# Four more products by C on GpSimd, its operands set 8 bytes apart, and a new order of the work around them

## The chip, the cores and the metric

The kernel runs on one core of a Trainium2 chip. The metric is the device time of one execution in microseconds (us). The engines that matter here are TensorE (PE in the profile), VectorE (DVE), ScalarE (ACT), GpSimd (POOL) and the queue that issues DMAs (SP). They run side by side and wait for each other on semaphores.

## What is computed

A layer of a state space model on images (8 images, 96 channels, 64x64), then attention and a feed forward layer. The change touches the selective scan alone:

```
dA = exp(dt * A)                     # per channel d (192) and state n (16)
h  = dA * h + (dt * u) * B           # step by step over 4096 places
y  = sum over n of h * C  + D * u    # for 4 directions, k = 0..3
```

Directions 2 and 3 go through the places backwards. `dt` is a softplus of a small projection of `u`; `B` and `C` are other rows of that projection.

## The kernel before

The function is `phase_scan`. The 192 x 16 rows of states make 24 **tiles** of 128 partitions, and the 4096 places are cut into 4 chunks of `T` = 1024 places: 8 images x 4 directions x 4 chunks = 128 **chunks** of 24 tiles. Each engine has its own hand-written order of a chunk (`body`, `run`, `rest`), which is the same for all chunks but for the ends; nothing schedules it at build time.

What happens to tile i of a chunk:

- ACT makes `exp` of it (`expo`, line 888) into one of two PSUM halves `pd[:, i % 2]`, two tiles ahead of the scan.
- GpSimd multiplies `dt * u` by B (`drive`, line 1103) into a ring of four buffers `dBu`. For the six *turned* tiles 9 to 14, ACT scales (line 929) and TensorE transposes (`turn_back`, line 796) instead, and `exp` goes straight into `h`.
- DVE runs the recurrence (`scan`, line 1063), with the last column of the chunk before from `carry`, which ACT saved (line 896).
- The result is multiplied by C. For 12 tiles DVE does it (`weigh`, line 1072), reading `pd`; for the other 12, called kept (each third tile and the turned ones), the scan writes to one of six places of `h`, and GpSimd multiplies there (`weigh`, line 1111), one element beside itself.
- TensorE adds up the states of three tiles at a time (`reduce_states(j)`, line 816, j = 0 to 7) into `py`, which ACT copies out after j = 3 and j = 7 (`copy_y`, line 963).

Woven into this, for the next chunk: the projection (`make_x_dbl` 746, its transposes `turn_b` 754, `make_step` 764), the softplus in ACT steps (`absolute` 935, `exp_abs` 939, `relu` 944, `one_plus` 948, `log` 953), its sum on TensorE (`add_up` 772 to 777), `dt * u` on DVE (`delta_u`, line 1044, after tiles 10 and 20), and its transposes (`turn_du` 784). The table `STEPS` says after which tile ACT does what, `SCALE` and `SCALE_NEXT` how many of the 32 scalings go after which tile. All of it is first in, first out on each engine, so what waits holds up all that is behind it.

In the profile, line 1103 reads `rep` and `BB` (in `shared`), line 1111 reads `h` and `CC` (in `shared`). The tensors `shared`, `rep`, `h` and `dBu` begin at multiples of 16 bytes. A place of `h` has 1025 elements of 4 bytes, so the six places begin at different offsets within 16 bytes; `rep`, `BB` and `CC` rows all begin at offset 0.

Of the kernel before, what the change touches and what calls it, by code (L numbers as in the profile page):

```python
# [17 lines left out]
F32 = mybir.dt.float32  # L18
# [5 lines left out]
L = H * W  # L24
# [354 lines left out]
def phase_scan(nc, a):  # L379

    with ExitStack() as ctx:
# [3 lines left out]
        BK = B * K  # L385

# [17 lines left out]
        BB = a.shared[:, 6 * T:9 * T].rearrange("p (r t) -> p r t", r=3)  # L404
        CC = a.shared[:, 9 * T:13 * T].rearrange("p (r t) -> p r t", r=4)
        hC_shared = a.shared[:, 13 * T:16 * T].rearrange("p (i t) -> p i t", i=3)
# [3 lines left out]
        hC_own = sb("hC", [128, 3, T])  # L410
# [17 lines left out]
        DRIVEN, WEIGHED, TURNED, SCALED = 18, 12, 6, 4 * TB  # L428
# [12 lines left out]
        KEPT = tuple(i for i in range(NS) if TRIPLES[i // 3][1] == 3 or i % 3 == 2)  # L441
# [5 lines left out]
        def kept(i, k):  # L447

            return h[:, KEPT.index(i) % 6, 1:T + 1] if k < 2 else h[:, KEPT.index(i) % 6, 0:T]

        def kept_last(i, k):

            return h[:, KEPT.index(i) % 6, T:T + 1] if k < 2 else h[:, KEPT.index(i) % 6, 0:1]

        def weighted(i, k):

            if is_kept(i):
                return h[:, KEPT.index(i) % 6, 0:T] if k < 2 else h[:, KEPT.index(i) % 6, 1:T + 1]
            slot = place(i) // 3 % 3 * 2 + i % 3
            return hC_own[:, slot, :] if slot < 3 else hC_shared[:, slot - 3, :]  # L460
# [5 lines left out]
        def saved_before(bk, c, i):  # L466

            before = KEPT.index(i) - 6
            if before >= 0 and c < NC - 1:
                return [carries(bk, c, KEPT[before])]  # L470
            return [carries(bk, c - 1, KEPT[before])] if before < 0 and c > 0 else []

        def kept_reduced(n, i):

            before = KEPT.index(i) - 6
            return (n + before // 12) * 8 + KEPT[before % 12] // 3 + 1

        def weighted_reduced(n, i):

            before = place(i) - 9  # L480
            return (n + before // DRIVEN) * 8 + tile_at(before % DRIVEN) // 3 + 1
# [8 lines left out]
        def place(i):  # L490

            j = i // 3
            return (j if j < 3 else j - 2) * 3 + i % 3
# [14 lines left out]
        def weighed_dve(n, i):  # L508

            return n * WEIGHED + place(i) // 3 * 2 + i % 3 + 1  # L510

        def weighed_pool(n, i):

            return n * WEIGHED + (1, 2, 3, 6, 9, 10, 11, 12)[i // 3] - (2 - i % 3 if is_turned(i) else 0)
# [77 lines left out]
        def _(sp):  # L592
# [42 lines left out]
            def load_c(m, s, r):  # L635
                sp.wait_ge(S.bc_stored, done((m + 1) * 16))
                sp.sem_inc(S.passed, 1)
                last = 3 * TRIPLES.index((1, r)) + 2
                if r < 3:
                    sp.wait_ge(S.hc_dve, done(weighed_dve(m - 1, last - 1)))  # L640
                    sp.sem_inc(S.passed, 1)
                sp.wait_ge(S.hc_pool, done(weighed_pool(m - 1, last)))
# [94 lines left out]
        def _(pe):  # L737
# [70 lines left out]
            def reduce_states(n, k, j):  # L808
                if j % 4 == 0:
                    pe.wait_ge(S.y_made, done(n * 2 + j // 4))  # L810
                if not is_turned(3 * j):
                    pe.wait_ge(S.hc_dve, done(weighed_dve(n, 3 * j + 1)))
                pe.wait_ge(S.hc_pool, done(weighed_pool(n, 3 * j + 2)))
# [18 lines left out]
            def body(bk, k, c, left):  # L832
# [4 lines left out]
                reduce_states(n, k, 1)  # L837
                turn_back(bk, c, 9)
                turn_back(bk, c, 10)
                reduce_states(n, k, 2)  # L840
# [5 lines left out]
                turn_back(bk, c, 14)  # L846
                if left:
                    make_step(n + 1, 1)
                skip(n, s, 0)
                reduce_states(n, k, 3)  # L850
# [4 lines left out]
                reduce_states(n, k, 5)  # L855
                if left:
                    turn_du(n + 1, 1)
                reduce_states(n, k, 6)
                if left >= 2:
                    make_x_dbl(n + 2, s)  # L860
                    turn_b(n + 2)
                    make_step(n + 2, 0)
                reduce_states(n, k, 7)
# [3 lines left out]
        def _(act):  # L867
# [107 lines left out]
            for i in range(2):  # L975
# [5 lines left out]
            STEPS = {0: [(absolute, 0)],  # L981
                     1: [(exp_abs, 0)],
                     2: [(relu, 0), (one_plus, 0)],
                     4: [(log, 0)],
                     9: [(copy_delta, 0)],
                     10: [(copy_du, 0)],
                     13: [(absolute, 1), (exp_abs, 1)],
                     14: [(relu, 1), (one_plus, 1)],
# [3 lines left out]
            SCALE = {0: 3, 2: 1, 3: 2, 4: 4, 5: 3, 6: 6}  # L992
            SCALE_NEXT = {20: 4, 21: 4, 23: 5}

            def run(bk, k, c, left, first, steps):
                n, s = bk * NC + c, c % 2
                for i in steps:
# [94 lines left out]
        def _(pool):  # L1092
# [24 lines left out]
            def body(bk, k, c, left):  # L1117
                n = bk * NC + c
                for j in range(8):
                    if is_turned(3 * j):  # L1120
                        for i in range(3 * j, 3 * j + 3):
                            weigh(n, k, i)
                    else:
                        p = place(3 * j) + 3
                        if left or p < DRIVEN:
                            for g in range(3):
                                drive(n, c, p + g)
                        weigh(n, k, 3 * j + 2)
# [670 lines left out]
def program(nc, a):  # L1799

    names = SEMAPHORES.split()
    with ExitStack() as ctx:
# [6 lines left out]
        a.shared = ctx.enter_context(nc.sbuf_tensor("shared", [128, 4 * L], F32))  # L1809
# [70 lines left out]
```

## Time and profile before

| | |
|---|---|
| median of three runs | 11818.88 us (11809.55 to 11828.68) |
| the profiled execution | 11838.25 us, of which the span in the trace is 11836.4 us |
| stage of the scan, 128 chunks | 849 to 10256 us of the span |
| busy in the span | PE 78%, DVE 90%, ACT 72%, GpSimd 75% |

The profile is one execution. A row of a timeline gives the start in us of the span, the time taken, engine, line, operation and tiles, and in brackets the idle time before it and who ended it. Instructions of one engine overlap slightly, so the time from start to start is what adds up. In rows that give stretches, PEclk is the granted clock of TensorE: 1.00 is 2.4 GHz and 0.50 is 1.2 GHz.

### The profile page before, as it was taken

The numbers are of one execution on the slowest core, as the hardware profiler recorded it, in microseconds if no ns is written. First come the engines' busy times: TensorE is split into PE (matmuls) and PEld (weight loads), VectorE is DVE, ScalarE is ACT, GpSimd is POOL, SyncE is SP. The second block draws the span as 40 slices with busy tenths as digits, with TensorE's granted clock in tenths as the row PEclk, the third lists the DMA queues.
The fourth block names the chain that finished last, engine by engine and source line by source line (L and its number), as shares of the span: only waits on it lengthen the run. The fifth ranks groups of instructions, "written<-read, shape, count | busy, mean of one in ns | idle before, by whom it ended". The sixth has DMA issues, their size and how long they took to land. (4 is left out here: it accounts for less than half of the span.)

```text
span 11836.4 us, 143180 instructions
## 1 busy us (share of the span) xinstructions
PE 9269.9 (78%) x34584; PEld 3297.3 (28%) x34584; DVE 10602.0 (90%) x6847; ACT 8553.0 (72%) x13829; POOL 8919.1 (75%) x3956
## 2 busy tenths in 40 slices
PE   8877777777777777777777777777777777588888
PEld 2322222222222222222222222222222222133333
DVE  7769999999999999999999999999999999866565
ACT  6767777777777777777777777777777777455555
POOL 0019998999899989998999899989999999521210
PEclk9988888888888888888888888888888888799898
DMA  3347777777777777777777777777777777644341
GB/s 106 118 131 183 182 184 178 183 183 184 178 182 184 182 174 183 184 179 175 187 183 183 177 184 182 178 177 184 183 182 182 187 180 180 147 111 99 93 106 48
DMA packets 577591, 1948.34 MB, mean 165 GB/s; under 512 B 106615, under 2 KB 111639, under 8 KB 562199
## 3 DMA queue, kind: packets, MB, share of 16 engines
q1 hardware_dynamic: 573714, 1938.65, 68.6%
q8 instruction: 265, 4.34, 0.2%
q14 instruction: 536, 4.38, 0.1%
q10 hardware_dynamic: 3076, 0.97, 0.1%
HBM read 1532.38 MB, written 406.85 MB: 164 GB/s over the span
## 5 line engine op out<-in xcount | busy, mean ns | idle before, releaser
L1103 POOL TENSOR_TENSOR dBu<-rep,shared 128x1024 f32<-128x1024 f32 x2304 | 5373.1, 2357 | 886.7 <-DMA rep<-dd_dram 832.1
L1111 POOL TENSOR_TENSOR h<-h,shared 128x1024 f32<-128x1024 f32 x1536 | 3310.3, 2162 | 717.5 <-DVE h L1063 700.7
L888 ACT ACTIVATE pd<-rep,a_now 128x1024 f32<-128x1024 f32 x2304 | 2566.7, 1114 | 761.1 <-DVE h L1063 463.0
L816 PE MATMUL py<-h,fold 128*32 128x512 f32 x6144 | 2613.6, 722 | 163.6 <-ACT y L963 163.6
L1063 DVE TENSOR_TENSOR_SCAN pd<-pd,carry,dBu 128x1024 f32<-128x1024 f32 x1152 | 2697.4, 2341 | 23.4 <-ACT pd L888 23.4
L816 PE MATMUL py<-hC,fold 128*32 128x512 f32 x3072 | 1366.7, 806 | 557.9 <-POOL h L1111 557.0
L929 ACT ACTIVATE shared<-shared,turned_b 128x192 f32<-128x192 f32 x4096 | 1528.1, 442 | 15.5 <-ACT shared L916 5.4
L816 PE MATMUL py<-shared,fold 128*32 128x512 f32 x3072 | 1409.9, 836 | 126.9 <-POOL h L1111 126.6
L1063 DVE TENSOR_TENSOR_SCAN h<-pd,carry,dBu 128x1024 f32<-128x1024 f32 x576 | 1349.5, 2343 | 103.3 <-ACT carry L896 53.1
L796 PE MATMUL pd<-eye,shared 128*128 128x128 f32 x6144 | 859.2, 288 | 597.9 <-DVE h L1063 402.4
L1063 DVE TENSOR_TENSOR_SCAN h<-h,carry,pd 128x1024 f32<-128x1024 f32 x576 | 1306.7, 2323 | 12.8 <-PE pd L796 6.9
L1072 DVE TENSOR_TENSOR hC<-pd,shared 128x1024 f32<-128x1024 f32 x768 | 940.5, 1225 | 81.5 <-DVE pd L1063 28.8
L1072 DVE TENSOR_TENSOR shared<-pd,shared 128x1024 f32<-128x1024 f32 x768 | 940.6, 1225 | 46.2
L796 PEld LDWEIGHTS pd<-eye,shared 128*128 128x128 f32 x6144 | 701.5, 145 | 913.0 <-DVE h L1063 501.3
L1063 DVE TENSOR_TENSOR_SCAN pd<-pd,dBu 128x1024 f32<-128x1024 f32 x384 | 876.1, 2282 | 47.8 <-issue 34.4
L888 ACT ACTIVATE h<-rep,a_now 128x1024 f32<-128x1024 f32 x768 | 846.7, 1140 | 15.2 <-ACT carry L896 10.3
L1782 POOL TENSOR_TENSOR shared<-shared 96x1024 f32<-96x1024 f32 x56 | 140.1, 2530 | 946.3 <-DMA shared<-y_dram 946.3
L764 PE MATMUL pp<-xdbl,w_dt 38*96 38x512 f32 x1024 | 716.2, 836 | 58.3 <-ACT turned_b L909 57.4
L916 ACT ACTIVATE shared<-pp 128x768 f32<-128x768 f32 x256 | 207.5, 810 | 638.5 <-PE pp L784 638.5
L816 PEld LDWEIGHTS py<-hC,fold 128*32 128x32 f32 x3072 | 230.7, 130 | 1476.3 <-POOL h L1111 688.4
L816 PEld LDWEIGHTS py<-h,fold 128*32 128x32 f32 x6144 | 449.8, 123 | 584.4 <-issue 466.3
L896 ACT ACTIVATE carry<-pd 128x1 f32<-128x1 f32 x1152 | 192.8, 167 | 577.1 <-DVE hC L1072 320.8
(174 smaller groups left out, 14520.0 us busy)
## 6 DMA issues: line engine op xcount, KB each, us to landing
rep<-dd_dram SPq DMA_DIRECT2D x1024, 768.0 KB, 12.3
shared<-bc_dram SPq DMA_DIRECT2D x3584, 128.0 KB, 5.8
u<-u_dram SPq DMA_DIRECT2D x128, 768.0 KB, 7.8
dd_dram<-LG SPq DMA_DIRECT2D x256, 384.0 KB, 4.6
dd_dram<-RL SPq DMA_DIRECT2D x256, 384.0 KB, 3.3
y_dram<-y SPq DMA_DIRECT2D x256, 384.0 KB, 7.3
shared<-y_dram SPq DMA_DIRECT2D x63, 1536.0 KB, 15.9
u_dram<-shared SPq DMA_DIRECT2D x32, 1536.0 KB, 7.5
```

The lines of the kernel that those rows point to most:

```text
L764: last = mm(pp[0:HALF, t2(t)], w_dt[:, half * HALF:(half + 1) * HALF], xdbl[:, t2(t)], start=True, stop=True)
L796: last = nc.tensor.transpose(pd[:, i % 2, block_of(q)], turned_dbu[:, q, half * 3 + g, :, :], eye128[:, :])
L816: last = mm(py[32 * g:32 * g + 32, t2(t)], fold[:, :], weighted(3 * j + g, k)[:, t2(t)], start=(j % 4 == 0), stop=(j % 4 == 3), skip_group ...
L888: go(dst, rep[:, half, 0, g, :], ACT.Exp, scale=a_now[:, column(i)]).then_inc(S.exped, 1)
L896: go(carry[:, i:i + 1], kept_last(i, k) if is_kept(i) else pd[:, i % 2, last_of(k)], ACT.Identity).then_inc(S.carried, 1)
L916: go(turned_du[:, :, 3 * half:3 * half + 3, :], pp[:, :].rearrange("p (q x) -> p q x", x=128)[:, :, 0:HALF].rearrange("p q (g d) -> p q g ...
L929: go(turned_dbu[:, q, :, j, :], turned_du[:, q, :, :], ACT.Identity, scale=turned_b[:, s, q, j:j + 1]).then_inc(S.scaled, 1)
L1063: v.tensor_tensor_scan(turned(state(i, k), k), turned(decay, k), turned(drive, k), first, ALU.mult, ALU.add).then_inc(S.scanned, 1)
L1072: v.tensor_tensor(weighted(i, 0), pd[:, i % 2, :], CC[:, r, :], ALU.mult).then_inc(S.hc_dve, 1)
L1103: nc.gpsimd.tensor_tensor(dBu[:, ring(c, p), :], rep[:, half, 1, g, :], BB[:, r, :], ALU.mult).then_inc(S.dbu, 1)
L1111: nc.gpsimd.tensor_tensor(turned(weighted(i, k), k), turned(kept(i, k), k), turned(CC[:, r, :], k), ALU.mult).then_inc(S.hc_pool, 1)
L1782: last = nc.gpsimd.tensor_tensor(Y[:, 0, c * T:(c + 1) * T], Y[:, 0, c * T:(c + 1) * T], Y[:, 2, c * T:(c + 1) * T], ALU.add)
```

## The change

- **Offsets.** `BB` moves by 2 elements (8 bytes), `CC` and the product buffers by 4, `shared` grows by 8 elements. A place of `h` has 1028 elements, and forward the scan writes from element 3 and the product from element 2 (backwards the other way round), so all places have the same offset.
- **Split.** `DVE_TILES` = 0, 3, 4, 6, 15, 18, 19, 21: DVE multiplies these 8 by C, GpSimd the other 16.
- **Places.** `h` has 8 places in place of 6; DVE's products have 4 in place of 6.
- **Order.** The orders of GpSimd, TensorE and ACT are written anew. On TensorE `reduce_states` 1 and 2 go behind other transposes, 5 goes behind `turn_du`, and 6 behind `make_x_dbl`, `turn_b` and `make_step` of the chunk after next. On ACT `absolute` and `exp_abs` of the first half go one tile later, `exp_abs` now right behind `copy_y`; `relu` of the second half goes one tile earlier.

```
-        KEPT = tuple(i for i in range(NS) if TRIPLES[i // 3][1] == 3 or i % 3 == 2)
+        DVE_TILES = (0, 3, 4, 6, 15, 18, 19, 21)
+        KEPT = tuple(i for i in range(NS) if i not in DVE_TILES)
...
-        BB = a.shared[:, 6 * T:9 * T].rearrange("p (r t) -> p r t", r=3)
-        CC = a.shared[:, 9 * T:13 * T].rearrange("p (r t) -> p r t", r=4)
+        BB = a.shared[:, 6 * T + 2:9 * T + 2].rearrange("p (r t) -> p r t", r=3)
+        CC = a.shared[:, 9 * T + 4:13 * T + 4].rearrange("p (r t) -> p r t", r=4)
...
-        h = sb("h", [128, 6, T + 1])
+        h = sb("h", [128, PLACES, T + 4])
...
-            return h[:, KEPT.index(i) % 6, 1:T + 1] if k < 2 else h[:, KEPT.index(i) % 6, 0:T]
+            return h[:, KEPT.index(i) % PLACES, 3:T + 3] if k < 2 else h[:, KEPT.index(i) % PLACES, 2:T + 2]
...
-            STEPS = {0: [(absolute, 0)],
-                     1: [(exp_abs, 0)],
-                     2: [(relu, 0), (one_plus, 0)],
+            STEPS = {1: [(absolute, 0)],
+                     2: [(exp_abs, 0), (relu, 0), (one_plus, 0)],
...
-                     13: [(absolute, 1), (exp_abs, 1)],
-                     14: [(relu, 1), (one_plus, 1)],
+                     12: [(absolute, 1), (exp_abs, 1)],
+                     13: [(relu, 1)],
+                     14: [(one_plus, 1)],
```

TensorE in the middle of a chunk, from the transposes of tile 13 to the sum of tiles 9 to 11 (`pd` is turned tiles, 764 `make_step`, 804 the skip term, 816 the sums). Before:

```order
L796 MATMUL pd<-eye,shared 128x128 x8
L790 REGISTER_ALU
L796 MATMUL pd<-eye,shared 128x128 x8
L764 MATMUL pp<-xdbl,w_dt 96x512 x2
L802 ISA
L804 MATMUL py<-u,w_skip 96x512 x2
L816 MATMUL py<-h,fold 32x512 x6
```

Now (the same lines are 799, 767, 807 and 821):

```order
L799 MATMUL pd<-eye,shared 128x128 x8
L767 MATMUL pp<-xdbl,w_dt 96x512 x2
L793 REGISTER_ALU
L799 MATMUL pd<-eye,shared 128x128 x8
L805 ISA
L807 MATMUL py<-u,w_skip 96x512 x2
L818 REGISTER_ALU
L816 REGISTER_ALU x2
L821 MATMUL py<-hC,fold 32x512
L821 MATMUL py<-h,fold 32x512 x2
```

The step goes ahead of the transposes of tile 14, and the sum of tiles 6 to 8 (the last two rows, and again for the other half of the places) stands ahead of that of 9 to 11.

TensorE at the end of a chunk, from `make_x_dbl` on to the last sum of the chunk, that of tiles 21 to 23. Before:

```order
L746 MATMUL pp<-u,w_x 38x512 x4
L751 REGISTER_ALU
L754 MATMUL pp<-eye,xdbl 128x38 x8
L764 MATMUL pp<-xdbl,w_dt 96x512 x2
L812 REGISTER_ALU
L816 MATMUL py<-shared,fold 32x512 x2
L816 MATMUL py<-h,fold 32x512
```

Now:

```order
L749 MATMUL pp<-u,w_x 38x512 x4
L754 REGISTER_ALU
L757 MATMUL pp<-eye,xdbl 128x38 x8
L767 MATMUL pp<-xdbl,w_dt 96x512 x2
L818 REGISTER_ALU x2
L816 REGISTER_ALU
L821 MATMUL py<-shared,fold 32x512 x2
L821 MATMUL py<-h,fold 32x512
L821 MATMUL py<-shared,fold 32x512 x2
L821 MATMUL py<-h,fold 32x512
L818 REGISTER_ALU
L816 REGISTER_ALU x2
L821 MATMUL py<-hC,fold 32x512
L821 MATMUL py<-h,fold 32x512 x2
```

Two sums stand behind the step now: that of tiles 18 to 20 (`shared` twice, `h` once) and, behind it, that of 21 to 23; before it was the last alone.

ACT around `copy_y` of the chunk before (963, now 968), after tile 2. Before:

```order
L888 ACTIVATE pd<-rep,a_now 128x1024
L961 REGISTER_ALU
L962 ISA
L963 ACTIVATE y<-py 96x1024
L942 ISA
L944 ACTIVATE RL<-pp,b_dt 96x1024
L948 ACTIVATE W<-E 96x1024
L929 ACTIVATE shared<-shared,turned_b 128x6x32
```

Now:

```order
L893 ACTIVATE pd<-rep,a_now 128x1024
L967 ISA
L968 ACTIVATE y<-py 96x1024
L944 ACTIVATE E<-E 96x1024
L947 ISA
L949 ACTIVATE RL<-pp,b_dt 96x1024
L953 ACTIVATE W<-E 96x1024
L934 ACTIVATE shared<-shared,turned_b 128x6x32 x2
```

One step of softplus (944) and one more scaling (934) now stand between `copy_y` and the next `exp` of a tile, that of tile 5.

## Rows read from the trace of the kernel before

**Rows 1.** The page, busy time, share of the span and instructions of each engine

```profile
PE 9269.9 (78%) x34584; PEld 3297.3 (28%) x34584; DVE 10602.0 (90%) x6847; ACT 8553.0 (72%) x13829; POOL 8919.1 (75%) x3956
```

**Rows 2.** Stretches: length, busy PE, PEld, DVE, ACT, POOL, then PEclk, DMA share, GB/s

```profile
849.00:10256.00 9407.00, 7242.45 (x28577) 2563.06 (x28580) 9049.02 (x4858) 7141.50 (x11774) 8635.37 (x3834) 0.87 0.77 181
...
3631.74:3703.89 72.15, 55.31 (x224) 19.80 (x224) 71.09 (x39) 56.67 (x99) 67.73 (x30) 0.91 0.78 183
7992.85:8068.27 75.42, 58.40 (x224) 20.06 (x224) 71.09 (x39) 57.04 (x99) 67.76 (x30) 0.84 0.76 179
```

**Rows 3.** DVE idle before its scans: releaser, us in total, times

```profile
  ACT pd L888: 98.8, 49
  ACT carry L896: 79.4, 31
...
  PE pd L796: 12.8, 24
```

**Rows 4.** Timeline of DVE, scans of tiles 1 to 3 of a chunk

```profile
3635.45 2.35 DVE L1063 TENSOR_TENSOR_SCAN pd<-pd,carry,dBu 128x1024 f32<-128x1024 f32 x1
...
3638.98 2.34 DVE L1063 TENSOR_TENSOR_SCAN h<-pd,carry,dBu 128x1024 f32<-128x1024 f32 x1
3641.24 2.33 DVE L1063 TENSOR_TENSOR_SCAN pd<-pd,carry,dBu 128x1024 f32<-128x1024 f32 x1
```

**Rows 5.** GpSimd by line: duration ns min/median/max

```profile
L1111 POOL TENSOR_TENSOR h<-h,shared x1536: 1907/2186/2404, 852.9 to 10252.0; 128x1024 f32<-128x1024 f32 x192
...
L1103 POOL TENSOR_TENSOR dBu<-rep,shared x2304: 2329/2356/2407, 832.5 to 10240.4; 128x1024 f32<-128x1024 f32 x192
```

**Rows 6.** Timeline of GpSimd, tile 5 of a backward chunk, tiles 2 to 5 of a forward one

```profile
1519.71 1.93 POOL L1111 TENSOR_TENSOR h<-h,shared 128x1024 f32<-128x1024 f32 x1
1521.60 7.00 POOL L1103 TENSOR_TENSOR dBu<-rep,shared 128x1024 f32<-128x1024 f32 x3
...
3641.40 2.34 POOL L1111 TENSOR_TENSOR h<-h,shared 128x1024 f32<-128x1024 f32 x1 [0.56 <-DVE h L1063]
3643.70 6.98 POOL L1103 TENSOR_TENSOR dBu<-rep,shared 128x1024 f32<-128x1024 f32 x3
3650.78 2.00 POOL L1111 TENSOR_TENSOR h<-h,shared 128x1024 f32<-128x1024 f32 x1
```

**Rows 7.** Timeline of PE over the end of a chunk at 3703.89

```profile
3694.73 1.32 PE L784 MATMUL pp<-eye,RL 96*128 96x96 f32 x8 [3.90 <-DVE RL L1044]
...
3705.43 3.73 PE L764 MATMUL pp<-xdbl,w_dt 38*96 38x512 f32 x4 [0.46 <-ACT turned_b L909]
3709.09 1.07 PE L816 MATMUL py<-shared,fold 128*32 128x512 f32 x2
...
3711.64 0.79 PE L816 MATMUL py<-shared,fold 128*32 128x512 f32 x2
```

**Rows 8.** Timeline of ACT behind it, and DVE's scan of tile 5

```profile
3714.54 1.00 ACT L963 ACTIVATE y<-py 96x1024 f32<-96x1024 f32 x1
...
3720.49 2.34 DVE L1063 TENSOR_TENSOR_SCAN h<-pd,carry,dBu 128x1024 f32<-128x1024 f32 x1
```

**Rows 9.** Timeline of PE in the middle of two chunks, and DVE's wait in the second

```profile
3671.24 1.95 PE L764 MATMUL pp<-xdbl,w_dt 38*96 38x512 f32 x4
3673.12 1.96 PE L804 MATMUL py<-u,w_skip 96*96 96x512 f32 x4
3675.01 1.92 PE L816 MATMUL py<-h,fold 128*32 128x512 f32 x12
...
8032.32 2.80 PE L764 MATMUL pp<-xdbl,w_dt 38*96 38x512 f32 x4
...
8046.13 2.35 DVE L1063 TENSOR_TENSOR_SCAN h<-pd,carry,dBu 128x1024 f32<-128x1024 f32 x1 [3.28 <-ACT carry L896]
```

**Rows 10.** Stretches of rows 7 and 9, columns as in rows 2

```profile
3705.50:3709.10 3.60, 3.60 (x7) 0.90 (x7) 3.38 (x3) 2.72 (x6) 3.60 (x3) 0.50 1.03 200
...
3670.30:3677.00 6.70, 6.63 (x28) 2.30 (x28) 6.58 (x3) 4.30 (x5) 6.53 (x4) 1.00 1.01 215
```

More of the change, by code:

```diff
@@ L466, in saved_before @@
         def saved_before(bk, c, i):
[L468 removed]
+            before = KEPT.index(i) - PLACES
             if before >= 0 and c < NC - 1:
@@ L637, in load_c @@
                 sp.sem_inc(S.passed, 1)
[L638 to L642, printed above, removed]
+                last = 3 * TRIPLES.index((1, r))
+                for i in range(last, last + 3):
+                    if not is_kept(i):
+                        sp.wait_ge(S.hc_dve, done(weighed_dve(m - 1, i)))
+                        sp.sem_inc(S.passed, 1)
+                sp.wait_ge(S.hc_pool, done(weighed_pool(m - 1, last + 2)))
                 sp.sem_inc(S.passed, 1)
@@ L810, in reduce_states @@
                     pe.wait_ge(S.y_made, done(n * 2 + j // 4))
-                if not is_turned(3 * j):
-                    pe.wait_ge(S.hc_dve, done(weighed_dve(n, 3 * j + 1)))
-                pe.wait_ge(S.hc_pool, done(weighed_pool(n, 3 * j + 2)))
+                for i in range(3 * j, 3 * j + 3):
+                    if is_kept(i):
+                        pe.wait_ge(S.hc_pool, done(weighed_pool(n, i)))
+                    else:
+                        pe.wait_ge(S.hc_dve, done(weighed_dve(n, i)))
                 for t in range(2):
@@ L991, in _, with run @@
                      20: [(copy_du, 1)]}
-            SCALE = {0: 3, 2: 1, 3: 2, 4: 4, 5: 3, 6: 6}
-            SCALE_NEXT = {20: 4, 21: 4, 23: 5}
-            def run(bk, k, c, left, first, steps):
+            SCALE = {0: 3, 2: 2, 3: 3, 4: 2, 5: 6, 6: 2, 7: 1}
+            SCALE_NEXT = {20: 5, 21: 3, 22: 2, 23: 3}
+            def run(bk, k, c, left, first, span):
                 n, s = bk * NC + c, c % 2
-                for i in steps:
+                for i in span:
                     if c < NC - 1:
@@ L1118, in body @@
                 n = bk * NC + c
[L1119 to L1128, printed above, removed]
+                drive(n, c, 3)
+                drive(n, c, 4)
+                weigh(n, k, 1)
+                weigh(n, k, 2)
+                drive(n, c, 5)
+                drive(n, c, 6)
+                drive(n, c, 7)
+                drive(n, c, 8)
+                weigh(n, k, 5)
+                drive(n, c, 9)
+                drive(n, c, 10)
+                weigh(n, k, 7)
+                drive(n, c, 11)
+                weigh(n, k, 8)
+                weigh(n, k, 9)
+                weigh(n, k, 10)
+                weigh(n, k, 11)
+                weigh(n, k, 12)
+                weigh(n, k, 13)
+                weigh(n, k, 14)
+                drive(n, c, 12)
+                drive(n, c, 13)
+                weigh(n, k, 16)
+                weigh(n, k, 17)
+                drive(n, c, 14)
+                drive(n, c, 15)
+                drive(n, c, 16)
+                drive(n, c, 17)
+                weigh(n, k, 20)
+                if left:
+                    drive(n, c, 18)
+                    drive(n, c, 19)
+                weigh(n, k, 22)
+                if left:
+                    drive(n, c, 20)
+                weigh(n, k, 23)
             chunk_loop(pool, body)
```

43 lines of the change are left out of this document (22 added, 21 removed).

## The prediction

> **What bounds the kernel now.** I read the busy shares first. DVE is busy 90% of the span, more than any other [rows 1], and in the stage of the scan, 9407 us or 73.5 us for each of its 128 chunks, 9049 us [rows 2]. An undisturbed chunk takes 72.15 us, with DVE busy for 71.1 of them [rows 2]: there DVE is the bound and waits for nobody. Other chunks take 75.42 with the same work. The idle time before the scans says how much that is: 98.8 and 79.4 us ended by ACT, 12.8 by PE [rows 3], together 191 us or 1.5 us for each chunk. So a chunk is DVE's work and 1.5 us of waits. GpSimd is busy 67.7 of 72.15 us, which leaves no room for four more products as they are.
>
> From start to start, a kept tile costs DVE 2.26 us and a tile with a product 3.53 [rows 4]; 3.58 on the mean, since 72.15 is 12 of these, 12 at 2.25 and two `delta_u` at 1.11.
>
> **GpSimd's times.** The multiplication by C has a shortest time of 1907 ns and a median of 2186, the one by B none under 2329 [rows 5]. The timeline shows two values, not a spread: tile 5 of a backward chunk takes 1.93, of a forward one 2.00, tile 2 takes 2.34 [rows 6]. Over the chunks that I followed, places 1, 2 and 5 of `h` always have the short time and places 0, 3 and 4 the long one. With 1025 elements to a place, the first begin in the other 8 bytes of 16 than C does (offsets 2, 3 and 2 against 0), the others in the same (1, 0 and 1). `rep` and `BB` both begin at 0 and have the long time. The change gives all places the offset of place 2, which is in the trace, and B the offset 2 against 0. From start to start a long one costs 2.33 (6.98 for three) and a short one 1.89 to 1.95 (from 1519.71 to 1521.60, from 3650.78 with 2.00 less the usual overlap) [rows 6]. So GpSimd's chunk becomes 34 x 1.92 = 65.3 us, with 63.5 for the least and 66.5 for the most. That multiplications by B become short too is the one part that no row shows; their operands differ from those of the short products only in which of the two is displaced, and I give it nine in ten.
>
> GpSimd is slower than DVE at this: the trace has 1.9 to 2.35 us against 1.22 for the same product. The Trainium skill says the same (GPSIMD Engine Reference, section 3.1), and gives about 2.5 cycles for each element as the floor with two inputs, since both are read through one port; 1024 elements at 1.2 GHz would be 2.13 us, an estimate from that page. The trace disagrees, with 1.907. By that rule the multiplications by B would end at 2.13, GpSimd's chunk at 34 x 2.13 = 72.5, and nothing would be gained.
>
> **DVE.** Four tiles less with a product: 4 x (3.58 - 2.26) = 5.3 us; an unhindered chunk is 66.9 us. With 128 chunks that is 675 us, if all else keeps pace. GpSimd does: its new order gives each buffer over 2 us or more before the scan that needs it, when I lay both orders side by side with these times. The places are no limit either: tile 16 is the earliest to need a sum of its own chunk (that of 6 to 8), and 3 has to wait for the old sum of 18 to 20, taken up below.
>
> **The end of a chunk is what I doubt.** PE's chain there starts with DVE's `delta_u` after tile 20. Its transposes start at 3694.73, the step at 3705.43, 10.7 us later; the last sum runs from 3709.09 to 3712.43 [rows 7], 8.5 us after the chunk's start at 3703.89. `copy_y` takes it at 3714.54 [rows 8], so 2.1 us are to spare. After the change, tiles 21 to 23 and `delta_u` take 1.11 + 3.58 + 2 x 2.26 = 9.2 us (10.5 now), so the chain starts 8.05 us before the chunk ends instead of 9.2. The step then starts at 2.65, and two sums follow it in place of one. The clock during the step is 0.50, 1.2 GHz, after PE had waited [rows 10], and the step takes 3.66, a sum 3.34 [rows 7]. At that clock the last sum ends at 2.65 + 3.66 + 2 x 3.34 = 13.0; at 2.4 GHz, with 1.88 and 1.9 [rows 9], at 8.3. I take 12.2, since the sums themselves may lift the clock before the last is done, as in the half of the last sum in rows 7 (its last group takes 0.79 us, not 1.07).
>
> ACT wants it after the `exp` of tile 4, at 8.2 + 1.1 = 9.3. From `copy_y` to the scan of tile 5 there then stand 0.9 (`copy_y`), 3 x 0.97 (`exp_abs`, `relu`, `one_plus`), 0.7 (two scalings), 0.25 (saves), 1.1 (`exp`) and 0.4 to the scan, 6.3 us. Today it is 5.95, of which part is slack [rows 8]. DVE wants tile 5 at 15.2. So it waits 0.4 us if the sum is early, 4.2 if all is at 1.2 GHz, and with 12.2 + 0.15: **3.4 us**. Tile 3's product waits for the first of the two sums, which ends at 9.65 where it is wanted at 10.6: free. From there on ACT is full up to tile 9 (32 scalings less 13 made before), and PE has stood still and may be at 1.2 GHz at the transposes of tiles 10 and 11 with a sum between them: **0.5 us**, between 0 and 1.5, of the size that a single wait for PE has today (12.8 us in 24) [rows 3]; the end at 1.5 is three of them.
>
> **The middle of a chunk.** Tile 17 needs `exp`, which stands behind `copy_y` of the first half, which needs the sum of tiles 9 to 11. From the end of scan 11 PE has then two sets of transposes (2 x 1.03), the step (1.88), the skip term (1.89) and two sums (3.8): 9.6 us, and from there to the scan 3.85 (`copy_y`, `one_plus`, saves, `exp`; `relu` is out of the way now), 13.5. DVE comes from there to tile 17 in 4 x 2.25 + 3.58 + 2.26 - 2.32 = 12.5. **1.0 us** of waiting in each chunk, even at 2.4 GHz. Before, this chain just fitted at 2.4 GHz [rows 9, 10] and cost 3.28 us where the clock fell (the step took 2.80 at 8032.32) [rows 9]. What the fall will cost then I put at **0.8 us** for the mean chunk, against 1.5 now: PE's long idle time before this stretch is gone, since the sum of tiles 3 to 5 and the step stand between the transposes now.
>
> **The sum.** 66.9 + 3.4 + 0.5 + 1.0 + 0.8 = 72.6 us, against 72.15 + 1.5 = 73.65. 1.05 us less, 128 times: 135 us, and 1.1%. Against the profiled execution, 11838 - 135 = 11703. The median of the runs is 19 us under it: 11684, of which I make 11680. Four fifths of what DVE saves are paid back in waits, if I am right, and one fifth remains.
>
> **Rivals.**
>
> *The cover holds.* If PE is at 2.4 GHz at the chunk's end, or its chain is faster than I lay it, `copy_y` costs 0.4 and not 3.4. Then a chunk is 66.9 + 0.4 + 0.3 + 1.0 + 0.5 = 69.1, 4.5 less: 580 us, 11240 us. For it: every term of the wait is a small difference of long chains, and with shorter chunks PE has less idle time. Against it: 0.50 in rows 10 after a shorter idle time than will be there.
>
> *The middle breaks, slower.* The chain in the middle has one more sum than before ahead of `copy_y`. If the clock falls there, its 7.5 us of step, skip and sums take up to twice that, and 3.3 to 6.6 us are added to the 1.0. It decides the sign from 1.85 us on the mean chunk instead of 0.8, so if about two chunks in five are hit with 4.6. With half of them hit, and 4.2 at the chunk's end: 66.9 + 4.2 + 0.5 + 1.0 + 2.5 = 75.1, 1.45 more, 12005 us. For it: 75.42 us chunks with 0.84 [rows 2] show that the clock does fall there. Against it: PE stood still ahead of it, and will less.
>
> *The operands do not do it.* If the products by B stay at 2.33: 18 x 2.33 + 16 x 1.92 = 72.7 us for GpSimd, which becomes the bound; with the hand-overs between it and DVE, 73 to 75 us, 11730 to 11990, say 11840. The 2.13 of the skill's page would end in the same place.
>
> **How the numbers follow.** The forecast, 11480 to 11800, has 0.45; the cover 0.25; the middle 0.17; the operands 0.08; the last 0.05 are for a give-back that just eats the gain. 0.2% of the time, 24 us, is about what a measurement of this kernel tells from no change. Faster is the first two, 0.70; slower the middle and half of the operands, 0.21; the same 0.09. The range reaches into the first rival to 11300 and into the second to 11930, with about 0.1 left out on either side.
>
> **What would show it.** The step that all rests on is GpSimd: lines 1108 and 1116 near 1.93 to 2.00 us, without a second value. DVE should have 1024 products of 1.22 us. Its idle time before scans should grow from 1.5 to some 5 or 6 us for each chunk, ended by ACT, in two places: before tile 5, with ACT having waited for PE's last sum at `copy_y`, and before tile 17. If chunks are near 69 us and `copy_y` waits for nothing, the first rival is right; if the wait before tile 17 is over 4 us in half of the chunks and the clock low there, the second; if DVE waits for `dBu`, the third. I would be wrong altogether if DVE were held by an engine that I have with room: SP's loads of C, or GpSimd's last product of a chunk.

## The result, and the profile after

| | before | changed |
|---|---|---|
| median of four runs each, us | 11822.52 (11809.55 to 11828.68) | 11701.33 (11682.28 to 11725.06) |
| ratio | | 0.9895 (0.9877 to 0.9912) |
| span of the profiled execution, us | 11836.4 | 11685.8 |

121 us less, 1.05%. The forecast was 11680, in a range of 11480 to 11800. Lines move by 5: the scan is 1068 now, DVE's product by C 1077, GpSimd's products 1108 and 1116, the sums 821, `copy_y` 968.

The page's first part, answering to [rows 1]: DVE has lost 566 us of work, and GpSimd, with 512 products more, 147 us.

```profile
PE 9207.4 (79%) x34584; PEld 3443.5 (29%) x34584; DVE 10036.1 (86%) x6335; ACT 8437.5 (72%) x13829; POOL 8772.1 (75%) x4468
```

GpSimd by line, duration in ns min/median/max, answering to [rows 5]. The products by B have come from 2356 to 1997 on the median, and those by C, of which half took 2.33 us and more, are all short:

```profile
L1108 POOL TENSOR_TENSOR dBu<-rep,shared x2304: 1986/1997/2077, 834.0 to 10106.9; 128x1024 f32<-128x1024 f32 x192
L1116 POOL TENSOR_TENSOR h<-h,shared x2048: 1917/1987/2026, 844.0 to 10116.5; 128x1024 f32<-128x1024 f32 x187
```

DVE's idle time before its scans (releaser, us, times), answering to [rows 3]: 664 us, where it was 231 (191 ended by ACT and PE, as in the prediction, and 40 "issue").

```profile
  ACT pd L893: 418.9, 265
  POOL dBu L1108: 120.6, 67
  PE pd L799: 55.3, 93
  ACT carry L901: 47.4, 78
  issue: 21.5, 33
```

Sorted by tile, 381 us of it, 3.0 for each chunk, stand before tile 5: 289.2 under ACT's `pd` and 92.0 under GpSimd's `dBu`. One such chunk begins at 5264.94. TensorE at its start, with the step, the sum of tiles 18 to 20 and the last sum (the rows from 5275.50 on), answering to [rows 7]:

```profile
5256.78 1.51 PE L787 MATMUL pp<-eye,RL 96*128 96x96 f32 x8 [4.27 <-DVE RL L1049]
...
5268.66 3.73 PE L767 MATMUL pp<-xdbl,w_dt 38*96 38x512 f32 x4 [1.25 <-ACT turned_b L914]
5272.32 1.07 PE L821 MATMUL py<-shared,fold 128*32 128x512 f32 x2
...
5274.88 0.78 PE L821 MATMUL py<-shared,fold 128*32 128x512 f32 x2
5275.50 0.59 PE L821 MATMUL py<-hC,fold 128*32 128x512 f32 x1
...
5276.78 0.59 PE L821 MATMUL py<-hC,fold 128*32 128x512 f32 x1
```

ACT behind it, from `copy_y` to `exp` of tile 5, answering to [rows 8]:

```profile
5277.54 1.02 ACT L968 ACTIVATE y<-py 96x1024 f32<-96x1024 f32 x1 [2.58 <-PE py L821]
5278.46 1.05 ACT L944 ACTIVATE E<-E 96x1024 f32<-96x1024 f32 x1
5279.41 1.10 ACT L949 ACTIVATE RL<-pp,b_dt 96x1024 f32<-96x1024 f32 x1
5280.41 1.05 ACT L953 ACTIVATE W<-E 96x1024 f32<-96x1024 f32 x1
5281.35 0.79 ACT L934 ACTIVATE shared<-shared,turned_b 128x192 f32<-128x192 f32 x2
...
5282.32 1.12 ACT L893 ACTIVATE pd<-rep,a_now 128x1024 f32<-128x1024 f32 x1
```

And GpSimd's four products 5 to 8, whose first has ended by 5277.9, with DVE's scan of tile 5:

```profile
5275.87 7.87 POOL L1108 TENSOR_TENSOR dBu<-rep,shared 128x1024 f32<-128x1024 f32 x4
...
5283.81 2.35 DVE L1068 TENSOR_TENSOR_SCAN h<-pd,carry,dBu 128x1024 f32<-128x1024 f32 x1 [3.12 <-POOL dBu L1108]
```

The sum ends at 5277.4, 12.4 us into the chunk; ACT has waited 2.58 us for it and needs 6.3 us more until the scan. The row blames GpSimd, but its product for tile 5 had been ready for 5.9 us: it is ACT's `exp`, which ended at 5283.44. In all 30 waits before tile 5 that are put down to GpSimd, ACT's `exp` ended 0.2 to 0.4 us before the scan began, so the 92 us are of the same wait.

Stretches, columns as in [rows 2]: that chunk, its step at the clock's lower level, 1.2 GHz, its middle (tile 12 to 17) and that of the chunk at 3012.44, one of two in which the clock fell there:

```profile
5264.94:5336.82 71.88, 55.85 (x225) 21.21 (x224) 66.74 (x36) 55.66 (x98) 65.98 (x35) 0.88 0.78 184
5268.66:5272.39 3.73, 3.73 (x7) 1.03 (x10) 3.57 (x3) 3.70 (x9) 3.73 (x3) 0.50 1.04 199
5302.43:5315.60 13.17, 11.56 (x61) 4.41 (x62) 12.53 (x7) 9.85 (x15) 12.16 (x7) 1.00 0.80 172
3050.52:3066.98 16.46, 14.85 (x61) 5.62 (x62) 12.64 (x8) 10.28 (x17) 13.65 (x7) 0.79 0.92 185
```

Below, "hit" is such a chunk: over 1.5 us more than its least between the scans of tiles 12 and 17. I count them among the 119 chunks that don't begin a batch of 16, the last chunk left out (all hits have a clock under 1.00 there): 31 before, 2 after.

### The profile page after: what moved, and what is told of

Same layout as the page of the kernel before. It is cut to its first block and busy times, and to the rows that moved or that the text cites. A ratio compares the mean times of both kernels' runs of the same rounds, so it can differ in the third digit from the quotient of the medians.

```text
span 11685.8 us, 144402 instructions
## 1 busy us (share of the span) xinstructions
PE 9207.4 (79%) x34584; PEld 3443.5 (29%) x34584; DVE 10036.1 (86%) x6335; ACT 8437.5 (72%) x13829; POOL 8772.1 (75%) x4468
## 5 line engine op out<-in xcount | busy, mean ns | idle before, releaser
L1108 POOL TENSOR_TENSOR dBu<-rep,shared 128x1024 f32<-128x1024 f32 x2304 | 4552.5, 1998 | 886.2 <-DMA rep<-dd_dram 833.5
L1116 POOL TENSOR_TENSOR h<-h,shared 128x1024 f32<-128x1024 f32 x2048 | 4020.7, 1972 | 728.6 <-DVE h L1068 728.0
L821 PE MATMUL py<-h,fold 128*32 128x512 f32 x8192 | 2447.8, 701 | 214.9 <-ACT y L968 214.9
L1068 DVE TENSOR_TENSOR_SCAN h<-pd,carry,dBu 128x1024 f32<-128x1024 f32 x960 | 2242.4, 2344 | 409.7 <-ACT pd L893 280.0
L1068 DVE TENSOR_TENSOR_SCAN pd<-pd,carry,dBu 128x1024 f32<-128x1024 f32 x768 | 1795.8, 2338 | 0.1
L1068 DVE TENSOR_TENSOR_SCAN h<-pd,dBu 128x1024 f32<-128x1024 f32 x320 | 729.2, 2284 | 139.5 <-ACT pd L893 88.7
L787 PE MATMUL pp<-eye,RL 96*128 96x96 f32 x2048 | 298.1, 307 | 559.5 <-DVE RL L1049 554.5
L1068 DVE TENSOR_TENSOR_SCAN pd<-pd,dBu 128x1024 f32<-128x1024 f32 x256 | 585.4, 2287 | 66.0 <-ACT pd L893 50.2
L775 PE MATMUL pp<-W,neg 97*96 97x512 f32 x1024 | 545.5, 614 | 106.5 <-ACT W L953 106.5
L968 ACT ACTIVATE y<-py 96x1024 f32<-96x1024 f32 x256 | 260.7, 1019 | 473.1 <-PE py L821 473.0
```

The costliest lines, as they stand in the source:

```text
L775: mm(pp[0:HALF, t2(t)], neg[:, :], W1[:, t2(t)], start=True, stop=False)
L787: last = nc.tensor.transpose(pp[:, q * 128:q * 128 + HALF], du[:, block_of(q)], eye)
L821: last = mm(py[32 * g:32 * g + 32, t2(t)], fold[:, :], weighted(3 * j + g, k)[:, t2(t)], start=(j % 4 == 0), stop=(j % 4 == 3), skip_group ...
L968: go(y[:, :], py[0:HALF, :], ACT.Identity).then_inc(S.y_made, 1)
L1068: v.tensor_tensor_scan(turned(state(i, k), k), turned(decay, k), turned(drive, k), first, ALU.mult, ALU.add).then_inc(S.scanned, 1)
L1108: nc.gpsimd.tensor_tensor(dBu[:, ring(c, p), :], rep[:, half, 1, g, :], BB[:, r, :], ALU.mult).then_inc(S.dbu, 1)
```

## The experiments

My theory: GpSimd was made shorter by the offsets alone; DVE's work came down, and 3.0 us of what that saves are paid back before tile 5, because two sums now stand behind TensorE's step. Ratios are to the kernel before as it was measured beside each run, with 95% intervals; its median moved between 11823 and 11831 us, so a difference of two medians below is good to some 10 us. Waits and counts of hits are of the one profiled execution of each kernel.

| kernel | median us | ratio |
|---|---|---|
| changed | 11701 | 0.9895 |
| e3, kernel before with the offsets alone | 11823 | 0.9997 (0.9984 to 1.001) |
| e4, changed, B in the same half | 11856 | 1.0021 (1.0012 to 1.0031) |
| e1, changed, sums 5 and 6 back | 11497 | 0.9713 (0.9697 to 0.9729) |
| e2, changed, `exp_abs` early | 11645 | 0.9834 (0.9813 to 0.9855) |
| e7, e1 and e2 | 11450 | 0.9684 (0.9661 to 0.9706) |
| e5, changed, `copy_y` behind tile 5 | 11560 | 0.9780 (0.9756 to 0.9804) |
| e9, e1 and e5 | 11631 | 0.9836 (0.9816 to 0.9857) |
| e6, changed, sums 1 and 2 back | 12021 | 1.0158 (1.0137 to 1.0179) |
| e10, e7, first `copy_y` later | 11529 | 0.9745 (0.9723 to 0.9768) |
| e11, e7, 16 products added | 11661 | 0.9861 (0.9839 to 0.9883) |
| e12, e7, 8 products added | 11500 | 0.9730 (0.9705 to 0.9755) |
| e13, e12, 8 more at the end | 11468 | 0.9701 (0.9676 to 0.9725) |

### Is it the offsets, and does GpSimd bound?

The kernel before with the new offsets of `BB`, `CC`, the product buffers and `h`, and nothing else:

```
-        BB = a.shared[:, 6 * T:9 * T]
+        BB = a.shared[:, 6 * T + 2:9 * T + 2]
...
-        h = sb("h", [128, 6, T + 1])
+        h = sb("h", [128, 6, T + 4])
```

> The kernel before, with nothing but the offsets of the change: the split stays 12 to 12, and so do the orders and the six places. My theory, that the halves of the 16 bytes in which GpSimd's two operands begin set its time, and that GpSimd bounds nothing before the change: its products all take 1.9 to 2.1 us, its busy time falls from 8635 to near 7400 us in the scan's stage, and the time stays where it was, within 0.3% of 11820. A rival, that a shorter GpSimd also takes waits from DVE: up to 100 us less.

Its GpSimd rows, columns as above, then the scan's stage, columns as in [rows 2]:

```profile
L1103 POOL TENSOR_TENSOR dBu<-rep,shared x2304: 1986/1998/2013, 832.0 to 10208.5; 128x1024 f32<-128x1024 f32 x192
...
L1111 POOL TENSOR_TENSOR h<-h,shared x1536: 1909/1982/2005, 852.6 to 10221.3; 128x1024 f32<-128x1024 f32 x192
```

```profile
849.00:10256.00 9407.00, 7205.67 (x28580) 2559.88 (x28580) 9070.01 (x4867) 7138.56 (x11773) 7541.09 (x3834) 0.87 0.78 181
```

1094 us less of GpSimd's work than in [rows 2], and no time. As expected: it was not on the path. Hits are 25 where they were 31, and DVE's idle time before scans is 201 us where it was 231. The other way round, the changed kernel with B alone in the half of the other operand:

```
-        BB = a.shared[:, 6 * T + 2:9 * T + 2]
+        BB = a.shared[:, 6 * T:9 * T]
```

> The changed kernel with B alone moved back to offset 0, the offset of the other operand. My theory: the products by B take 2.33 us again and those by C 1.95 to 2.0, GpSimd's chunk is 18 x 2.33 + 16 x 1.97 = 73.5 us and it becomes the bound; DVE waits for dBu in every chunk, and the time is 11750 to 12000, say 11850. The rival, that the place of C alone sets both times or that the cause is not the offset: products by B stay near 2.0 and the time stays at 11700.

Its products by B, and the stage up to 10000:

```profile
L1108 POOL TENSOR_TENSOR dBu<-rep,shared x2304: 2327/2356/2464, 834.4 to 10254.9; 128x1024 f32<-128x1024 f32 x192
```

```profile
849.00:10000.00 9151.00, 7065.37 (x27805) 2645.29 (x27804) 8247.69 (x4225) 6847.88 (x11478) 9021.04 (x4223) 0.86 0.77 181
```

Two elements of offset are worth 155 us here. The products by B are at 2356 again, those by C stay at 1986, and GpSimd is busy 98.6% of the stage: it is the bound, 73.6 us a chunk. The prediction put this rival at 11840; it came at 11856. That DVE would be seen waiting for `dBu` was wrong: its idle time is 580.1 us under ACT's `pd`, before tiles 5 and 1, and 84.5 under `dBu`. GpSimd's lateness comes to it, at least in part, over TensorE's sums: they wait for GpSimd's products 126.0 us in 60 waits, where it was 47.1 in 10, ACT's wait for the projection behind one of them is 312.0 us where it was 189.5, and the last sum ends 13.9 us into the mean chunk and not 12.7.

### Is it the last sum that tile 5 waits for?

```
+                reduce_states(n, k, 5)
                 if left:
                     turn_du(n + 1, 1)
-                reduce_states(n, k, 5)
+                reduce_states(n, k, 6)
                 if left >= 2:
                     make_x_dbl(n + 2, s)
                     turn_b(n + 2)
                     make_step(n + 2, 0)
-                reduce_states(n, k, 6)
```

> The changed kernel with the sums 5 and 6 on TensorE where they stood before the change: sum 5 ahead of the transposes of dt * u, sum 6 right behind them and ahead of the projection. My theory, that DVE waits 3.0 us for each chunk before tile 5 because the last sum of the chunk before ends 12.4 us into the chunk, behind two others: that sum now ends near 9.7, and the wait falls to 0.4 to 0.7 us. 128 x 2.4 is 300 us less than the changed kernel, near 11400. A rival, that ACT is just full there and the sum only the last to be named: the wait moves to the next tile and the time stays near 11700. A second, that with the projection behind two sums its own result comes later than tile 1 of the next chunk wants it: the gain is halved, near 11550, with DVE waiting before tile 1 or 3 instead.

The same chunk of this kernel begins at 5162.10. The last sum follows the step at once:

```profile
5166.15 3.72 PE L767 MATMUL pp<-xdbl,w_dt 38*96 38x512 f32 x4 [1.25 <-ACT turned_b L914]
...
5172.37 0.63 PE L821 MATMUL py<-hC,fold 128*32 128x512 f32 x1
...
5173.16 1.02 ACT L968 ACTIVATE y<-py 96x1024 f32<-96x1024 f32 x1 [0.71 <-PE py L821]
...
5179.42 2.35 DVE L1068 TENSOR_TENSOR_SCAN h<-pd,carry,dBu 128x1024 f32<-128x1024 f32 x1 [1.24 <-ACT pd L893]
```

It ends 10.9 us into the chunk and not 12.4, and DVE waits 1.24 us, not 3.12. Over all chunks 156 us are left before tile 5 of 381: 226 less and not 300, since the sum at 1.2 GHz ends 1.2 us later than I had it. The time fell by 204, to 11497 and not to 11400: the waits before tiles 1, 17 and 14 grew by 33, 22 and 17 us, and hits rose from 2 to 16. So the second rival was right in a small part.

The next run leaves the sums where the change put them, and moves a step of ACT:

```
-            STEPS = {1: [(absolute, 0)],
-                     2: [(exp_abs, 0), (relu, 0), (one_plus, 0)],
+            STEPS = {1: [(absolute, 0), (exp_abs, 0)],
+                     2: [(relu, 0), (one_plus, 0)],
```

> The changed kernel with the first half's exp_abs after tile 1 again, ahead of copy_y, and not behind it. My theory: ACT stands still from 10.0 to 12.6 us of a chunk, waiting for the last sum, and exp_abs fits in there. One step of 0.95 us less lies between the sum and exp of tile 5, so the wait before tile 5 falls from 3.0 to near 2.05 us; 128 x 0.95 is 120 us less, near 11580. The rival, that ACT's work up to tile 9 bounds this part whatever its order: nothing, 11700.

From start to start tile 4 to 5 takes 5.70 us on the mean, not 6.57: 0.87 for each chunk, 110 us. But the time fell by 56 only (72 by the ratios), to 11645 and not to 11580. Hits rose from 2 to 17 of 119, and in the profiled execution the waits before tiles 11, 14, 16 and 17 grew by 17, 20, 12 and 31 us. So the step off the chain did what was expected, and about half of it or more was given back in the middle.

Both edits together:

> Sums 5 and 6 back as in the run with the sums alone (11497), and exp_abs of the first half ahead of copy_y as in the run with that alone (57 us less than the changed kernel). If the two act on one chain, from the last sum to exp of tile 5, the second takes 0.95 us or what is left of the wait: 60 to 110 us less than 11497, near 11410. If they act on different waits they add up to 11440. If the wait that remains before tile 5 in the run with the sums is not this chain, 11497.

11450, a little over the 11410 to 11440 that I had, and the best of all: 3.2% under the kernel before and 2.1% under the changed one. 71.9 us are left before tile 5 (50.5 under ACT's `pd`, 15.9 under TensorE's `py`, 4.1 under `dBu`, 1.5 "issue"), and the mean chunk takes 70.46 us. Again the time fell by less than the removed wait, 252 of 309 us: hits are 34 now. ACT takes the last sum without waiting for it here (0.03 us on the mean, 2.6 in the changed kernel), so what is left before tile 5 isn't the sum's any more.

### Is the place of the copy all that matters?

```
-                    if i == 2 and not first:
+                    if i == 3 and not first:
                         copy_y(n - 1, 1)
```

> The changed kernel with the copy of the old sums (copy_y of the second half) one tile later on ACT, so behind exp of tile 5 and not ahead of it. TensorE's order is as in the changed kernel. My theory, that the wait before tile 5 is nothing but that chain from the last sum over copy_y to exp: the wait of 3.0 us goes, and 0 to 0.5 comes back at tile 6 or behind it, since copy_y then starts near 12.6 as before and exp of tile 6 has 2.3 us more; 128 x 2.5 is 320 us less, near 11380. The rival, that ACT is full between tile 2 and tile 9 and the order in it does not matter: the wait turns up before tiles 6 to 11 and the time stays over 11600.

No wait is left before tile 5 (3.51 us from start to start), all 381 us gone, but the time fell by 142, to 11560 and not to 11380. DVE's idle time of this kernel:

```profile
  ACT pd L893: 215.0, 293
  PE pd L799: 135.0, 124
  ACT carry L901: 105.3, 78
  issue: 28.1, 46
  PE py L821: 15.2, 12
```

By tile, 88.9 us stand before tile 9 (12.2 in the changed kernel), 57.2 before 14 (1.6), 129.6 before 17 (52.5), 82.4 before 1 (56.7), 41.1 before 6 (none), and hits are 39. There is one `py` for both halves. So the next chunk's first sum can't start before `copy_y` has read it, and behind it in TensorE's order stand `add_up` and the transposes of tile 9: TensorE's sums wait 569.7 us for `copy_y`, where it was 388.3. My theory had the wait right and what lies behind it wrong.

> Both at once: sums 5 and 6 where they stood before the change, and copy_y of the second half behind exp of tile 5. The run with the sums alone still had 157 us of waits before tile 5, 1.2 us for each chunk (the last sum ended 10.9 us into chunk 61, since TensorE ran at 1.2 GHz). My theory: those go too, 11497 less 130 to 157 us, near 11350. If ACT or the projection's own chain (88 us of waits before tile 1) bounds, 11450 to 11500.

With the sum early as well it is slower than with either of the sums' or the copy's place alone (11497, 11560), and slower than either case that I had expected. TensorE's waits in this kernel, us in total, times, longest, from 849 to 10000 us:

```profile
PE py L821 <- ACT y L968: 788.8, 227, 10.5
...
PE pp L749 <- DMA u<-u_dram: 127.1, 81, 3.8
```

The first was 288.2 in the kernel with the sums alone, the second 41.2. `u` is loaded by SP when `skip` has been computed; the later `copy_y`, the later `skip`, the later `u`, and DVE waits 147 us before tile 1 (90 with the sums alone). That this chain of hand-overs is the cause I read from the order of the code and from these waits; no run tests it.

### The middle

```
+                reduce_states(n, k, 1)
                 turn_back(bk, c, 9)
                 turn_back(bk, c, 10)
-                reduce_states(n, k, 1)
+                reduce_states(n, k, 2)
                 turn_back(bk, c, 11)
...
-                reduce_states(n, k, 2)
```

> The changed kernel with sums 1 and 2 on TensorE where they stood before the change: 1 ahead of the transposes of tile 9, 2 between those of tiles 10 and 11. My theory for the wait before tile 17 (0.4 us for each chunk), that the sum of tiles 6 to 8 stands in the chain from scan 11 to copy_y of the first half: it goes, 50 us less; but transposes of tiles 11 and 9 come 2 to 3.5 us later, behind the sums, and DVE's wait for pd by TensorE before tiles 9 and 11 (0.4 us for each chunk) grows to 1 to 2. Together 11700 to 11850. The rival, that TensorE has the room before tile 9: near 11650.

No wait is left before tile 17, as I had it, and 405.5 us stand before tile 11, 369.6 of them under TensorE's `pd` (48.6 and 42.1 in the changed kernel). I gave these sums 1 to 2 us for each chunk; they cost 3.2, and the time, 12021, lies outside my 11700 to 11850. The old place is 2.7% worse. The clock is under 1.00 between tiles 12 and 17 in 35 of the 119 chunks of this kernel, and none of them is a hit: a lower clock by itself doesn't make one.

```
-                    if i == 14:
+                    if i == 15:
                         copy_y(n, 0)
```

> The kernel with sums 5 and 6 back and exp_abs early (11450), and copy_y of the first half one tile later, behind exp of tile 17 and no longer ahead of it. In that kernel DVE still waits 90 us before tile 17 for ACT's carry and 30 us for its exp. My theory: both waits are the chain over the sum of tiles 9 to 11 and copy_y to exp of tile 17; they go, and 60 to 120 us with them, to 11330 to 11390. The rival, learnt from the run in which copy_y of the second half went one tile later: the next sum on TensorE and add_up behind it wait for the copy, and the time comes back before tiles 21 to 1: 11450 or more.

The rival was right: tile 17's 119 us are gone, but 51.3 came before `delta_u`, 121.9 us stand before tile 1 where it was 64.4, and 35.0 before tile 23 where it was 6.8; 79 us more in all.

Now the clock. In some chunks it falls behind the transposes of tiles 11 and 12, of `dt * u` and of tile 13. Products that nobody reads (`fill`) go in between:

```
                 turn_back(bk, c, 12)
+                fill(8)
                 if left:
                     turn_du(n + 1, 0)
+                fill(8)
                 turn_back(bk, c, 13)
```

> The kernel with sums 5 and 6 back and exp_abs early (11450), and 16 products of 128x128 by fold added on TensorE, whose result nobody reads: 8 behind the transposes of tile 12 and 8 ahead of those of tile 13, where TensorE stands still for 1.4 and 1.5 us. In that kernel 34 chunks lose 3.9 us each between tiles 12 and 16, with a granted clock of 0.79 there and not 1.00, which is 1.0 us for the mean chunk. If the clock falls there because TensorE stands still in these gaps, the 34 become few and the time falls by 80 to 130 us, to 11320 to 11370. If it falls for what was before tile 9, or by itself, nothing is gained, and the products that do not fit the gaps cost up to 1 us a chunk: 11450 to 11570.

> As the run with 16 added products, with 4 and 4 of them in place of 8 and 8. There 8 took 1.93 us where TensorE had 1.4 to 1.5 us of room, the granted clock between tiles 12 and 16 was 1.00 in every chunk and no chunk lost over 1.5 us there, but DVE waited 208 us before tile 13 for transposes that came too late. 4 take 0.97 us and fit. If what holds the clock is that TensorE is at work in these two gaps, half of it may do: the 34 chunks that lost 3.9 us become few, nothing waits before tile 13, and the time is 11450 less 80 to 130 us, near 11340. If it takes all 16, the hits stay and the time is 11430 to 11470.

Tile 12 to 17, columns as in [rows 2]: a hit and the next chunk of e7.

```profile
3704.46:3720.85 16.39, 14.77 (x61) 5.60 (x62) 12.43 (x7) 10.25 (x17) 13.69 (x8) 0.79 0.88 185
3776.62:3789.78 13.16, 11.51 (x61) 4.40 (x62) 12.52 (x7) 10.23 (x17) 12.15 (x7) 1.00 0.82 176
```

A chunk with 16 products (e11):

```profile
3917.05:3932.92 15.87, 14.40 (x88) 6.76 (x86) 12.85 (x8) 10.92 (x17) 12.20 (x7) 1.00 0.86 181
```

And one with 8 (e12):

```profile
3860.46:3874.78 14.32, 12.85 (x74) 5.38 (x73) 12.86 (x7) 10.91 (x17) 12.21 (x7) 1.00 0.94 194
```

Of 34 hits none is left, with 16 products or with 8, and the granted clock is 1.00 there in every chunk. So the half of my expectations on the clock held, and the half on the time did not: e11 takes 211 us more than e7 (11661, where even my rival said 11570 at most), with 225 us of waits before tile 13 and 73 before tile 14, and e12 takes 50 us more, 11500 where I had 11340 or at most 11470. With 8 products the stretch takes 14.25 us on the mean, against 14.09 in e7. TensorE's timeline in that good chunk of e7, and then in the chunk with 8 products, shows why:

```profile
3773.20 1.97 PE L799 MATMUL pd<-eye,shared 128*128 128x128 f32 x16
3775.00 0.83 PE L787 MATMUL pp<-eye,RL 96*128 96x96 f32 x8
3776.75 1.09 PE L799 MATMUL pd<-eye,shared 128*128 128x128 f32 x8 [0.93 <-DVE h L1068]
```

```profile
3858.96 1.06 PE L805 MATMUL py<-eye,fold 128*32 128x128 f32 x8
3859.95 0.88 PE L787 MATMUL pp<-eye,RL 96*128 96x96 f32 x8
3860.76 1.06 PE L805 MATMUL py<-eye,fold 128*32 128x128 f32 x8
3861.75 1.09 PE L799 MATMUL pd<-eye,shared 128*128 128x128 f32 x8
```

The gaps of 1.4 and 1.5 us in my expectations were misread: ahead of the transposes of `dt * u` (787) there is none, ahead of those of tile 13 one of 0.93. The two groups of 4 products (8 matmuls each, 0.99 us from start to start) need 1.98 us, where 0.93 is free. So the transposes of tile 13, which start 0.13 us behind the scan of tile 12 (at 3776.62) in e7, start 1.29 behind it (at 3860.46) in e12, and that delay costs about what the hits had cost, 1.0 us for the mean chunk. By this sum one group alone would about fit; that wasn't tried.

The last run adds two groups at the chunk's end:

> As the run with 4 and 4 added products, and 4 more behind the projection (make_x_dbl) and 4 ahead of the step at the chunk's end, where TensorE stands still for 2.0 and 1.7 us before it takes 3.7 us for the step and 3.6 us for the last sum at 1.2 GHz. If the clock holds there as it did in the middle, the step and the sum take 1.9 us each, the last sum ends 3 us earlier, and the waits left before tiles 5 and 1 (60 and 54 us) mostly go: 60 to 110 us less than with 4 and 4. If the clock is low there for the copies that TensorE waits for at that place whatever it does, the same time, or up to 60 us more since the products delay turn_b.

One chunk of it begins at 5155.45. Its step, its last sum and ACT's `copy_y` behind them:

```profile
5159.27 1.95 PE L767 MATMUL pp<-xdbl,w_dt 38*96 38x512 f32 x4 [0.26 <-ACT turned_b L923]
...
5162.47 0.59 PE L826 MATMUL py<-hC,fold 128*32 128x512 f32 x1
...
5166.60 1.00 ACT L977 ACTIVATE y<-py 96x1024 f32<-96x1024 f32 x1
```

The clock did as I hoped: it is 0.98 over the step in the mean chunk (0.57 in e12), the step takes 2.0 us, and the last sum ends 8.0 us into the chunk and not 10.9. The waits did not: ACT comes to `copy_y` at 11.4 us (11.5 in e12), in both without waiting for the sum, 62 us stay before tile 5 (70 in e12) and 87 before tile 1 (85). So with the sums back and `exp_abs` early it is ACT's own work that tile 5 waits for, and a faster TensorE takes next to nothing off that wait. The time falls by 33 us from e12, half of the least that I expected and not where I expected it, and it doesn't beat e7.

## Why the prediction was right, point by point

- **GpSimd's offsets: right.** B became short too, the part that no row showed. I took 1.92 us from start to start; it is 1.96 by B (5264.26, 5266.22) and 1.92 by C, so a chunk is about 66 and not 65.3 (65.98 busy in the chunk shown), inside my bounds. The prediction's offsets of the places are those of the forward directions. Backwards the operands are read from their last element, and the halves are those of that element: place 1, read from offset 0 against 3, takes 1.93 us on the median, and place 3, read from 2 against 3, takes 2.35. Counted from the lowest address, both would come out the other way round. All 1536 products by C of the kernel before fit this.
- **The skill's rule.** GpSimd's two-input product took 1.99 us on the median, with its two operands in different halves, and 2.36 in the same. The floor of some 2.5 cycles for each element in the Trainium skill (GPSIMD Engine Reference, section 2.1, Instruction dispatch; section 3.1, which the prediction names for it, has some 2.6) would be 2.13 us at 1.2 GHz, an estimate from that page; the trace disagrees in all 4352 products, of which the longest took 2.08.
- **DVE: right in what is left, too large in what is saved.** With every wait over 0.15 us taken out, the mean chunk is 67.0 us, where I had 66.9. With 5.2 of idle time before scans (664 by 128, where I had 5.7) and 0.3 before its products this makes the mean chunk's 72.5. But the same measure gives 71.6 before, and waits of 2.0, where I had 72.15 and 1.5: I left out the 40 us of "issue" and 29 before products, and took the 72.15 of one chunk, with 0.24 of waits in it, for the mean chunk's own work. So the saving was 4.5 us and not 5.3, and the waits grew by 3.5 and not by 4.2. The two errors cancel, which is luck.
- **Before tile 5: right in place and cause, 3.4 expected, 3.0 measured.** The last sum ended at 12.4 in the chunk shown (12.7 in the mean chunk), where I had 12.2, and the clock rose during the first of the two sums (5274.88 is the first row of it that is shorter), as I had supposed it might. That it came out so near is in part luck: the step started 3.7 us into the chunk and not 2.65, since `turn_b` and the step waited 1.41 and 1.25 us for ACT, and the two sums took 5.0 us and not 5.9. From `copy_y` to the scan I had 6.3 us, and it took 6.3. e1, e2 and e5 each took the wait, or a part of it, away at another place of the same chain.
- **Tiles 8 to 11: right.** 0.5 expected, 71 us in 128 chunks measured, 49 of them before tile 11.
- **Tile 17: too large.** 1.0 expected, 0.4 measured (52.5 us). That the chain is there, e6 and e10 show: each takes the wait away at another end.
- **The clock in the middle: too large.** I put 0.8 on it, with the reason that the idle time before it is gone; it is 2 hits of 3 us, nearly nothing. The reason isn't shown: e1, e2, e7 and e5 have the same order of TensorE in the middle, and 16, 17, 34 and 39 hits.
- **What I did not have:** 0.4 us before tile 1 (`copy_x_dbl` waits for the projection, which now stands behind a sum), 0.2 before tile 23, and 0.3 before tile 15 (six chunks, the first of a batch). With 0.2 before tile 0 and 0.3 before DVE's products, both much as before, they make 1.5 us, against 1.7 that I had too much: that the mean chunk is 72.5 where the sum gave 72.6 is in part luck. The range held, and so did the cause of the largest term.
- **The rivals.** The cover did not hold: 3.0 before tile 5. The middle did not break here, but it does in e5 (39 hits of 4.4 us) and e7 (34 of 3.9): where the wait at the front is taken away, part of it comes back as a lower clock. Added products stop that. Why the changed kernel escapes it with the same work in the same order is open. The operands did it, and e4 shows what that rival would have cost. Open too is what the split brings with the old orders, or the new orders and eight places without it: no run separates them, but for the sums (e1, e6).

## What to carry to other kernels

When an engine with room is loaded up to relieve the one that bounds, lay out the whole chain of the engine that hands over between chunks. Here two thirds of the saving, 3.0 of 4.5 us, went into two sums set behind one step, and giving them their old place back was worth more than the change itself. A wait removed at one place of a FIFO engine is worth what is late next: 381 us taken away before tile 5 brought 142, with 181 us more of TensorE waiting for the buffer that the moved copy holds. And once nobody waits at the end of a chain, shortening it gives little: in e13 the last sum came 2.9 us earlier in each chunk, and 8 us went from the waits before tile 5 in all. And check that the engine named as the releaser had not been done long before.

## What the runs showed of the hardware

- GpSimd's product of two 128x1024 f32 operands in SBUF takes 1.99 us when they start in different 8-byte halves of 16 bytes, and 2.36 in the same: 15% less, for either of its two products and whichever operand is displaced. The halves count from the element that is read first, also when it is the last one. e3 and e4 change nothing but offsets.
- Behind some 4.6 us of transposes (3773.20 to 3777.78 above) with one gap of 0.9 us in them, TensorE's granted clock fell in 34 of 119 chunks of e7, and in none of e12, with twice 4 small products between them. In the changed kernel, with the same transposes and a gap of 1.31 us at 5302.56, it fell in 2. Whether it is the gap or the transposes or what went before that lets it fall, these runs do not tell apart. The Trainium skill (TensorE: Matmul & The Clock Gate, Part 4) says that a transpose does not count as work in the same way; no run here shows that by itself.
- The same products at the chunk's end (e13) lifted the clock over the step from 0.57 to 0.98 on the mean, and the step took 2.0 us and not 3.3. Products that nobody reads can hold the clock, but here they brought no time over e7: they cost as much where they stand in the way, or the faster work wasn't waited for.
